# Last stage of a fused two-layer network: tokens sorted by expert instead of every expert for every token

## The reference

```python
x = x + xattn_0(layernorm(x), ctx)          # stage l0 of the kernel
x = x + slots_ffn(layernorm(x))             # stages l0, sl (slots), la
x = x + perceiver(ctx, layernorm(x))        # stage pa, then the first half of stage ex:
#   out = layernorm(out @ Wout)             #   out: 512 x 1024 per batch, Wout: 1024 x 512
x = x + experts(layernorm(x))               # second half of stage ex

def experts(x):                             # 4096 tokens, 8 experts
    top1 = argmax(x @ Wg.T)                 # one expert for each token
    xhat = layernorm(x)
    for e in range(8):
        h = gelu((xhat * scale[e] + bias[e]) @ W1[e] + b1[e])   # 512 -> 128
        y += (top1 == e) * (h @ W2[e] + b2[e])                  # 128 -> 512
```

## Time and profile before

| | us |
|---|---|
| median of 3 runs | 3330.24 (3322.26 to 3330.74) |
| the profiled execution's own time | 3332.2 |
| its span, first to last instruction | 3330.4 |
| TensorE busy | 2998.8 (90%), 16620 matmuls |
| VectorE busy | 2078.5 (62%) |
| ScalarE busy | 1557.5 (47%) |
| GpSimd busy | 1324.4 (40%) |
| DMA | 220.43 MB, mean 66 GB/s |
| mean granted TensorE clock | 0.938 of full speed |

### The profile page before, as it was taken

The page is one execution under the profiler, slowest core; times in us unless marked ns, Lnnn a source line. Parts: engine busy times, 40 slices in busy tenths (PEclk is TensorE's granted clock), DMA queues, the critical chain, the costliest instruction groups (busy, mean ns, idle before and its releaser), DMA issues. The chain is left out here.

```text
span 3330.4 us, 44846 instructions
## 1 busy us (share of the span) xinstructions
PE 2998.8 (90%) x16620; PEld 2522.2 (76%) x16620; DVE 2078.5 (62%) x4123; ACT 1557.5 (47%) x3036; POOL 1324.4 (40%) x913
## 2 busy tenths in 40 slices
PE   6888999967675799999999999999999769999998
PEld 5777777745333798989899898989989657777776
DVE  4766666632357677777777777777777654444442
ACT  2333333321024576767767676777767522222222
POOL 2444444420012355565656565655555421111110
PEclk9999999987776899999999999999999879999999
DMA  5112111113059212121211212121121331111100
GB/s 181 36 46 60 51 49 40 47 38 139 0 189 365 79 41 60 37 63 40 62 34 36 65 36 63 38 70 31 38 63 34 107 101 51 51 51 51 51 26 26
DMA packets 131550, 220.43 MB, mean 66 GB/s; under 512 B 44749, under 2 KB 46798, under 8 KB 127245
## 3 DMA queue, kind: packets, MB, share of 16 engines
q1 hardware_dynamic: 120237, 187.42, 18.3%
q10 hardware_dynamic: 11104, 30.23, 2.3%
HBM read 112.01 MB, written 69.47 MB: 54 GB/s over the span
## 5 line engine op out<-in xcount | busy, mean ns | idle before, releaser
L1644 POOL TENSOR_SCALAR pa_Pr<-pa_Pr,pa_rs 128x590 f32<-128x590 f32 x512 | 903.1, 1768 | 647.5 <-DVE pa_rs L1866 647.4
L1870 DVE TENSOR_REDUCE pa_least<-pa_S 128x1 f32<-128x590 f32 x512 | 390.7, 763 | 192.0 <-PE pa_S L1708 189.8
L1821 DVE TENSOR_TENSOR pa_PTl<-pa_W,pa_PTh 128x512 fp32r<-128x512 f32 (+1 forms) x640 | 421.1, 683 | 26.1 <-ACT pa_PTh L1769 18.1
L1800 ACT ACTIVATE pa_Pr<-pa_S,pa_least 128x590 f32<-128x590 f32 x512 | 384.8, 752 | 100.3 <-DVE pa_least L1870 97.0
L1769 ACT ACTIVATE pa_PTh<-pa_W 128x512 fp32r<-128x512 f32 (+1 forms) x640 | 367.4, 596 | 115.1 <-PE pa_W L1719 98.4
L1719 PE MATMUL pa_W<-pa_ident,pa_Pr 128*128 128x128 f32 (+1 forms) x2560 | 365.5, 273 | 0.7 <-DVE pa_U L1821 0.6
L1719 PEld LDWEIGHTS pa_W<-pa_ident,pa_Pr 128*128 128x128 f32 (+1 forms) x2560 | 303.9, 142 | 23.3 <-DVE pa_U L1821 0.8
L1733 PE MATMUL pa_O<-pa_PTh,pa_V 128*128 128x512 f32 (+1 forms) x640 | 288.4, 451 | 12.3 <-DVE pa_PTl L1821 8.1
L1734 PE MATMUL pa_O<-pa_PTl,pa_V 128*128 128x512 f32 (+1 forms) x640 | 252.7, 395 | 0.0
L1706 PE MATMUL pa_S<-pa_U,pa_Qh 128*128 128x296 f32 (+1 forms) x1024 | 228.1, 304 | 5.5 <-DMA pa_Um<-pa_U 5.2
L1708 PE MATMUL pa_S<-pa_Um,pa_Ql 128*128 128x296 f32 (+1 forms) x1024 | 222.8, 299 | 0.0
(11 more groups left out here) (400 smaller groups left out, 7236.7 us busy)
## 6 DMA issues: line engine op xcount, KB each, us to landing
pa_Um<-pa_U SPq DMA_DIRECT2D x128, 147.5 KB
pa_Qh<-pa_Qh SPq DMA_DIRECT2D x128, 128.0 KB
o_s<-pa_O_pair SPq DMA_DIRECT2D x64, 256.0 KB, 2.6
ex_o_raw<-o_s SPq DMA_DIRECT2D x8, 2048.0 KB, 10.7
z_s<-la_z_hi ACTq DMA_DIRECT2D x8, 1180.0 KB, 7.2
z_s<-la_z_lo ACTq DMA_DIRECT2D x8, 1180.0 KB, 9.5
pa_z_hi<-z_s SPq DMA_DIRECT2D x8, 1180.0 KB, 5.7
pa_z_lo<-z_s SPq DMA_DIRECT2D x8, 1180.0 KB, 8.4
```

The costliest lines, as they stand in the source:

```text
L1644: pool.tensor_scalar(p, p, rs[:, g % 2, t:t + 1], None, ALU.mult).then_inc(*pool_s.mark("probs", n))
L1800: act.activation(Pr[g % 2][:, t, :], scored[n % 2], ACT.Exp, scale=-1.0, bias=least[:, g % 2, t:t + 1], accum_out=rs[:, g % 2, t:t + 1]).t ...
L1821: dve.tensor_tensor(out, src, f32(hi_ap), ALU.subtract).then_inc(*dve_s.mark(*name))
L1870: dve.tensor_reduce(least[:, g % 2, t:t + 1], scored[n % 2], AX, ALU.min).then_inc(*dve_s.mark("least", n))
```

## The change

Stage ex is built anew, in two phases, and two other stages are touched.

Phase 1 goes through the batches with read-out, norms and gate as before, but without experts. Each token's row (its normed x, its x with the residual, and its number, 1028 words) is scattered to a DRAM table `xs_s`, to the place in its expert's region. The place comes from two small matmuls and running counts (`ranks`, `running_counts`, `row_places`). The scatter is four indirect DMAs a batch on POOL (`send`), 128 rows of 4.1 KB each. The experts' weights are cut in eight chunks, one a batch, and stored to a second table `wt_s` (`load_chunk`, `store_chunk`). x has three buffers, o has one and a half. The load of x for batch b+1 waits until the rows of batch b-2 have been scattered.

Then `routes` (some thirty small VectorE steps) works out for 15 tiles which expert each has and where its rows lie.

Phase 2 goes through 15 tiles of 512 rows of one expert. For each, POOL fetches the expert's weights (128 x 2561 words, 1.3 MB) and the rows (128 x 4112 words, 2.1 MB; rows outside the region aren't fetched) with one indirect DMA each. TensorE transposes the rows (`row_columns`, 16 transposes), makes `first_product` (12 matmuls) and `second_product` (4 times 4 matmuls), and VectorE adds the rows (`result`). POOL scatters the result to `out` by four indirect DMAs. Rows and weights have four buffers each.

In stage pa, SP clears `xs_s` (68 MB in all) by one DMA of some 1.1 MB for each of the 64 head pairs, after the store of that pair's turn. In stage sl, slot_init and WhhT in three parts are loaded ahead of si, and the three `gh` products come ahead of the transposes of si.

```diff
@@ build_slots
-            sp.dma_start(WhhT[:, :, :], rows(a["Whh_T"])).then_inc(w_in["WhhT"], 16)
+            sp.dma_start(S0T[:, :, :], rows(a["slot_init_T"])).then_inc(S0_in, 16)
+            for n in range(3):
+                sp.dma_start(WhhT[:, :, n * D:(n + 1) * D], rows(a["Whh_T"])[:, :, n * D:(n + 1) * D]).then_inc(Whh_in[n], 16)
             sp.dma_start(si[:, :, :], si_s.rearrange("(j b) s d -> (b s) j d", j=NP)).then_inc(si_in, 16)
@@ build_perceiver, at the end of SP's turn for pair p
+                if n0 < whole:
+                    cleared += clear(n0, whole)
@@ build_experts, SP
+            def load_x(b):
+                if b >= 3:
+                    sp.wait_ge(free[b % 3], 16 * NT * (b // 3))
+                elif b > 0:
+                    w_cut(sp, 2)
+                sp.dma_start(R4[b % 3][:, :, D:2 * D], x2_s[b:b + 1].rearrange("b (t p) d -> p (b t) d", p=P)).then_inc(x_in[b % 3], 16)
...
             for b in range(B):
+                load_chunk(b)
+                if batch(b + 1):
+                    load_x(b + 1)
+                    load_o(b + 1)
+                store_chunk(b)
@@ build_experts, POOL
+            def send(b):
+                pool.wait_ge(*dve_s.after("place", b))
+                pool.wait_ge(*dve_s.after("xh", b, NT - 1))
+                pool.wait_ge(*pool_s.after("token", b))
                 for t in range(NT):
+                    pool.indirect_dma_start(xs_s, bass.IndirectOffsetOnAxis(ap=place[:, b, t:t + 1], axis=0), R4[b % 3][:, t, :], None)\
+                        .then_inc(free[b % 3], 16)
...
+            for i in range(NW - 1):
+                fetch_weights(i)
+            for n in range(3):
+                pool.wait_ge(free[n], 16 * NT * rows_out[n])
+            pool.wait_ge(*dve_s.after("src"))
+            for i in range(3):
+                fetch_rows(i)
+            for i in range(TILES):
+                pool.wait_ge(*dve_s.after("tok", i))
+                for j in range(NT):
+                    pool.wait_ge(*dve_s.after("free", "y", i, j))
+                    pool.indirect_dma_start(out_rows, bass.IndirectOffsetOnAxis(ap=tok[:, i, j:j + 1], axis=0), R4[buf(i)][:, j, D:2 * D], None,
+                                            bounds_check=TOKENS - 1, oob_is_err=False).then_inc(free[buf(i)], 16)
+                if tile(i + 3):
+                    fetch_weights(i + 3)
+                    fetch_rows(i + 3)
@@ build_experts, TensorE
+            for b in range(B + 2):
+                now, was = batch(b), batch(b - 1)
+                if now:
+                    read_out(b, 0)
+                    read_out(b, 1)
+                if batch(b - 2):
+                    ranks(b - 2)
+                if was:
+                    transposed(b - 1)
+                if now:
+                    read_out(b, 2)
+                if was:
+                    gate_logits(b - 1)
+                if now:
+                    shifts(b)
+                    read_out(b, 3)
+                if was:
+                    gate_rows(b - 1)
...
+            for i in range(TILES + 1):
+                first_product(i)
+                for j in range(NT):
+                    second_product(i - 1, j)
+                    row_columns(i + 1, j)
@@ build_experts, VectorE
+            for i in range(TILES + 1):
+                for j in range(NT):
+                    if tile(i - 1):
+                        result(i - 1, j)
+                    if j == 0 and tile(i):
+                        low(i)
+                    if tile(i + 1):
+                        transposed_lo("rT", i + 1, j)
```

More of the change, by code:

```diff
@@ L1067, in matmuls @@
                 return last
+            pe.wait_ge(S0_in, 16)
+            for n in range(3):
+                ps = unit("gh", n)
+                pe.wait_ge(Whh_in[n], 16)
+                for c in range(C):
+                    m = matmuls(ps[:, c * NS:(c + 1) * NS], WhhT, n * D + c * P, n * D + (c + 1) * P, S0T, 0, NS)
+                m.then_inc(*pe_s.mark("gh", n))
+            pe.wait_ge(si_in, 16)
             for c in range(C):
@@ L1073, in _ @@
                 m.then_inc(*pe_s.mark("siT", c))
-            pe.wait_ge(small, 16 * len(smalls))
-            pe.wait_ge(w_in["WhhT"], 16)
-            for n in range(3):
-                ps = unit("gh", n)
-                for c in range(C):
-                    m = matmuls(ps[:, c * NS:(c + 1) * NS], WhhT, n * D + c * P, n * D + (c + 1) * P, S0T, 0, NS)
-                m.then_inc(*pe_s.mark("gh", n))
             pe.wait_ge(w_in["WihT"], 16)
@@ L1889, in _, with build_experts @@
                     w_vector(dve, n + 7, n + 8)
[L1894 removed]
+def build_experts(nc, orders, a, o_s, x2_s, out, xs_s, wt_s):
     B, T, D = a["x"].shape
@@ L1952, in build_experts @@
+        table = sem("table")
+        free = [sem(f"free{n}") for n in range(4)]
+        rows_in, wt_in = [sem(f"rows_in{n}") for n in range(4)], [sem(f"wt_in{n}") for n in range(NW)]
         pe_s, act_s, dve_s, pool_s = (Marks(sem(n), orders) for n in ("products", "act", "dve", "pool"))
-        rows = lambda w: w.rearrange("(c p) n -> p c n", p=P)
-        weights, w2s = [], []
+        chunks = lambda w: w.rearrange("(c p) n -> p c n", p=P)
+        weights = []
         for n in range(2):
@@ L2061, in _ @@
+            for n in range(4):
+                used = len([i for i in range(TILES) if buf(i) == n])
+                pool.wait_ge(free[n], 16 * NT * (rows_out[n] + used))
         @block.tensor
@@ L2109, in shut @@
-            def shut(b, e):
-                pe.wait_ge(*dve_s.after("free", "hotT", b))
-                pe.matmul(bank_of["h", b, e][:, :], sel[:, e:e + 1].to_broadcast([P, HE]), hotT[:, :], start=False, stop=True).then_inc(*pe_s.mark("h", b, e))
-            def biases(b):
-                pe.wait_ge(small_cut, 2)
-                pe.wait_ge(*dve_s.after("free", "hotT", b))
-                for t in range(NT):
-                    ps = claim(pe, "out", b, t)
-                    pe.matmul(ps[:, :], hotT[:, t * P:(t + 1) * P], b2[:, :], start=True, stop=False)
@@ L2143, in _ @@
[L2143 to L2174 removed]
+                pe.matmul(ps[:, 0:NT * E], tri[:, :], hot[b % 2][:, :, :].rearrange("p t e -> p (t e)"), start=True, stop=False)
@@ new lines, in ranks, with shifts @@
+                pe.wait_ge(*pool_s.after("cum", b, NT - 1))
+                pe.matmul(ps[:, 0:NT * E], ones[:, :], cum[b % 2][:, :, :].rearrange("p t e -> p (t e)"), start=False, stop=True)\
+                  .then_inc(*pe_s.mark("rank", b))
+            def shifts(n):
+                if n < NCH // 2:
+                    ps = claim(pe, "shift", n)
+                    pe.wait_ge(small, 16 * len(smalls))
+                    pe.wait_ge(raw_in, 16 * (n + 1))
+                    for e in range(EC):
+                        for c in range(C):
+                            k = (n * EC + e) * C + c
+                            m = pe.matmul(ps[:, e:e + 1], raw[:, (e * C + c) * HE:(e * C + c + 1) * HE], shift[:, k:k + 1], start=(c == 0), stop=(c == C - 1))
+                    m.then_inc(*pe_s.mark("shift", n))
@@ new lines, in second_product @@
+            def second_product(i, j):
+                if not tile(i):
+                    return
+                w = Wt[i % NW]
+                ps = claim(pe, "y", i, j)
+                pe.matmul(ps[:, :], bias_rows[:, :], w[:, B2:B2 + D], start=True, stop=False)
+                pe.wait_ge(*dve_s.after("lo", i))
+                product(pe, ps[:, :], [z[:, j * P:(j + 1) * P] for z in h[i % 2]], [w[:, (2 + x) * D:(3 + x) * D] for x in range(2)], False, True)\
+                    .then_inc(*pe_s.mark("y", i, j))
@@ L2176, in _ @@
+            ps = claim(pe, "count")
+            pe.wait_ge(*pool_s.after("cum all"))
+            pe.matmul(ps[:, 0:E], ones[:, :], cum_all[:, :], start=True, stop=True).then_inc(*pe_s.mark("count"))
+            for c in range(C):
+                row_columns(0, c)
+            for i in range(TILES + 1):
[3 more added lines that the diff above has]
+                    row_columns(i + 1, j)
         @block.scalar
@@ new lines, in _ @@
+            act.wait_ge(small, 16 * len(smalls))
+            act.activation(Wg[0][:, :, :], Wg_raw[:, :, :], ACT.Copy).then_inc(*act_s.mark("Wg hi"))
+            act.activation(h[0][0][0:E, :], b2_raw[:, :], ACT.Copy).then_inc(*act_s.mark("b2 hi"))
+            for b in range(B + 1):
+                for k in range(K // 2, K):
+                    cut_o(b, k)
+                if batch(b - 1):
+                    for c in range(C):
+                        transposed_hi("xT", b - 1, c)
+                cut_o(b + 1, 0)
+                cut_o(b + 1, 1)
+                if batch(b - 1):
+                    act.wait_ge(*pe_s.after("LT", b - 1))
+                    act.activation(LT[:, :], bank_of["LT", b - 1][0:E, :], ACT.Copy).then_inc(*act_s.mark("free", "LT", b - 1))
+                cut_o(b + 1, 2)
+                cut_o(b + 1, 3)
```

(2 more changed lines are left out.)

715 lines of the change are left out of this document (409 added, 306 removed).

## The result

The changed kernel takes 3290.5 us (median of 4 runs, 3289.1 to 3294.7) against 3330.5 us for the kernel before beside it on the same chip: a ratio of 0.9887, 95% interval 0.9868 to 0.9905. It is faster, by 40 us; 3249 was forecast, a gain of 81. The profiled execution took 3290.5 us, its span is 3288.7.

A forecast was written before the change was run, and what follows sets the result against it. TensorE, 90% busy, was taken as the bound, stage ex a queue of matmuls. Stage ex end 3263 instead of 3330.4 (-67) and slots -14 gave 3251, 3249 at the median; range 3130 to 3345 us.

The forecast's parts named there:

- both chains: Phase 1: load of o behind scatters, 41.2 us a turn; phase 2: fetch behind scatters, 17.0 us a tile plus rows.
- Case B: Rival for both phases: indirect DMA cheap for POOL (p = 0.5) and the clock stays up; 3186 us, chance 0.26.
- C: Rival: nothing exposed, -61 us in phase 1 and -136 in phase 2; 3052 us, chance 0.07.
- D: Rival: POOL becomes the bound by its DMA issues, in phase 2's queue; 3386 us at p = 3.8, chance 0.14.
- E: Rival: indirect transfers run at half of 395 GB/s, rows taking over 15 us to land; 3336 us, chance 0.11.
- p: Time POOL takes to issue one indirect DMA, taken as 1.36 us, bounds 0.37 and 3.8.
- The low price for the issue: Estimate weighed for POOL's indirect DMAs: p at 0.4 and fixed part 2.0 us, the sum some 65 us lower.
- Phase 1, the new wait: Phase 1 from turn 2: loads of x and o wait for scatters; chain of 41.2 us, five times.
- term of 20.8 us for VectorE's own list: Phase 1 chain: VectorE's pieces of o, residuals, norms, choice, low half and small steps for places and shifts, 20.8 us.
- The start of the stage: Stage ex from its start to the first scatter, forecast at 91 us.
- The first chain: Phase 2 from its start to the landing of tile 3: tiles 0 to 2 at free pace, then one chain, 31 us.
- the tail: End of phase 2: two steps and the last scatter, 21.5 us.

The follow-up runs named there:

- experiments 1 and 2: 1: changed kernel, weights and rows fetched ahead of the scatters, 3187.7 us; 2: changed kernel, load of o ahead of load of x, 3242.3 us.
- experiment 6: Changed kernel with GpSimd's additions to x cut to one column instead of 512: 3270.6 us, ratio 0.9827.
- Experiment 10: Changed kernel with weights and rows fetched ahead of scatters, o loaded ahead of x, and VectorE's constants ahead of its first weight wait: 3134.1 us.
- experiment 7: Changed kernel with every fetch taking all 512 rows of its tile, unwanted ones too: 3312.7 us, ratio 0.9958.

## Why the forecast came out 40 us high in its gain

**The direction and the mechanisms were right.** TensorE's work left; both chains took its place, at the two places named; experiments 1 and 2 take each away alone and give back 103 and 48 us. Case B falls with its cheap issue; cases C, D and E fall too: something is exposed, GpSimd is 45% busy and not a bound, and full rows land after 10.3 to 10.8 us, not over 15.

**p was right, in part by luck.** The issues of an indirect DMA follow one another at 1.25 to 1.41 us (1.55 once), forecast 1.36, and with it the 58 us between the phases. But 1.36 was the length of an addition, a piece of work of another kind; nothing on record tied the two together. The Trainium skill ("DMA: Bandwidth & Descriptors", section Anatomy of one DMA) calls the generation of descriptors small. The low price for the issue that I weighed beside it is wrong: GpSimd spends 1.0 us on each. The same section of the Trainium skill puts the fixed part of a transfer at some 2.0 us, and the 2.3 us of the empty fetch, issue included, fit that better than my 3.1 plus an issue.

**The step that failed: "Phase 1, the new wait", in its term of 20.8 us for VectorE's own list.** It counted VectorE's passes by their durations before and GpSimd not at all, though GpSimd gives each residual its inverse root and had to do four additions of 1.36 in the same turn. I had the 42.5 us of that row before me and used it only as a price for p. The change had put them in front of the inverse root of the first residual. Measured: 45.1 a turn for 41.2, 19.7 us over five; experiment 6 puts 14.6 of them on the additions. The term itself came out at 24.4 us in each turn, with the first cut 0.7 that stands beside it, for 21.5; without the additions it is 21.4. Of the rest, 4.1 us are in the landing of the scatters, put at the 2.6 us of a plain store.

**The start of the stage** was the second: 103.8 us for 91. The first outer norm came 32.2 us after the start for 27.7. VectorE's constants, new in the change and costed at nothing, stood 6.65 us between two cuts of o. Turn 0 then lost 2.5 us more, turn 1 took 31.4 for 29, and turn 2 has the additions' wait again. Experiment 10 gives the constants 4 us, experiment 6 the additions 5. The rest is not settled.

**Phase 2 came out 7.7 us over by luck as much as by reckoning.** From landing to the next issue of rows 10.6 us were forecast, and 10.6 measured on average (10.0 to 11.5). From issue to landing the eleven chains took 98.4 us for 100.2 (11 times 6.4, and 29.8 of bytes): tiles 4, 7 and 8 took 0.7 to 2.6 us more than their bytes, as experiment 7 explains, the empty ones 0.7 to 1.2 less and those of 512 rows 1.1 to 1.4 less. The first chain (35.4 for 31) and the tail (25.9 for 21.5) are over by 4.4 each, which was not looked into; less the 1.8 by which the eleven chains were under, that is about the 7.7.

**Slots and clears** came out together by luck. The start of stage ex, 14.9 us earlier for 14 forecast, is a sum of parts that were off: 17 us won in the slots stage, the forecast's upper bound (a clock that is up sooner, as it said there), and some 3 us lost in the perceiver stage, where the 61 clears were put at nothing. The gap on SP covers a clear's own transfer; what they slow down was not looked into.

## What to carry to other kernels

A lead of n tiles is worth what stands between issue and need in each engine's order: fetch for the tile that is n ahead before you queue anything of the present tile, or the lead is one. After such a fix take the order apart again, since an edit that shortened the old chain can lengthen the new one (rows ahead of weights: 40 us gained, then 34 lost). And in a turn's sum, list what GpSimd does in it: work there is not free for VectorE even where nobody waits for it.
